# The third lane of the expert loop works its blocks from the last one backwards

## The reference

```python
x = x + L0_xattn(layernorm(x), ctx)      # 16 heads, 722 context rows
x = x + L0_ffn(layernorm(x))             # mixture of experts, below
x = x + L1_xattn(layernorm(x), ctx)
x = x + L1_ffn(layernorm(x))             # ternary weights, 4096 hidden

# L0_ffn: H=1024, E=32 experts, K=4 per token, I=512
logits = x @ gate_w.T + gate_b
topk_logits, topk_idx = top_k(logits, 4)
weight = softmax(topk_logits)
# for each (token, expert) pair:
gate, up = x @ w_gate[e] + b_gate[e], x @ w_up[e] + b_up[e]     # clipped at 7
act  = (up + 1) * gate * sigmoid(1.702 * gate)
y    = sum over the 4 experts of weight * (act @ w_down[e] + b_down[e])
```

## Time and profile before

| | us |
|---|---|
| median of 3 runs | 3518.92 (3517.94 to 3521.68) |
| the profiled execution's own time | 3516.27 |
| its span in the trace | 3514.5 |
| TensorE busy (PE) | 3425.6, 97% |
| VectorE busy (DVE) | 1634.5, 47% |

### The profile page before, as it was taken

How to read it: one execution, slowest core, us unless ns; L and a number is a source line. 1 busy time by engine, 2 the same in 40 slices (tenths; PEclk the granted TensorE clock), 3 DMA queues, 4 the chain that set the end, 5 groups by cost and what they waited for, 6 DMA issues and landing times.

```text
span 3514.5 us, 43051 instructions
## 1 busy us (share of the span) xinstructions
PE 3425.6 (97%) x16460; PEld 1797.4 (51%) x16461; DVE 1634.5 (47%) x1978; ACT 863.7 (25%) x1256; POOL 744.6 (21%) x709
## 2 busy tenths in 40 slices
PE   7999999999999789999999989999999999999999
PEld 4565565566456333333333346556565565554554
DVE  8764474565466431111111146446255365661651
ACT  2330131032023211111111125335154252220110
POOL 4200400400320012212222210000000002780860
PEclk9999999999999989999999999999999999999999
DMA  7631231132123196898888975436355251430420
GB/s 224 225 100 53 63 87 47 68 101 64 49 69 123 77 369 211 303 381 313 285 293 315 368 238 168 134 132 183 100 161 155 85 160 56 149 137 2 160 90 38
DMA packets 93173, 556.64 MB, mean 158 GB/s; under 512 B 11304, under 2 KB 11440, under 8 KB 74992
## 3 DMA queue, kind: packets, MB, share of 16 engines
q1 hardware_dynamic: 58432, 445.28, 35.5%
q0 software_dynamic: 31392, 93.76, 10.3%
q10 hardware_dynamic: 3216, 15.68, 1.5%
HBM read 517.62 MB, written 40.71 MB: 159 GB/s over the span
## 4 chain that ended last, share of the span: by engine, by line
PE 86%; DMA 4%; DVE 3%; ACT 1%; issue 1%; SPq 0%; POOL 0%; DVEq 0%; POOLq 0%; ACTq 0%
PE PS L967 15%; PE PS L1950 11%; PE PS L2284 10%; PE PS L1114 9%; PE PS L924 8%; PE PS L1974 6%; PE PS L2310 5%; PE PS L953 4%; DMA W<-in_W 4%; PE PS L819 4%; PE PS L836 3%; PE PS L903 2%; PE PS L1050 2%; PE PS L851 2%; PE PS L977 1%; PE PS L1942 1%
## 5 line engine op out<-in xcount | busy, mean ns | idle before, releaser
L967 PE MATMUL PS<-Sb,kvN 121*128 121x400 f32 (+1 forms) x1536 | 536.7, 499 | 0.0
L1950 PE MATMUL PS<-W,hT 128*64 128x512 f32 x2208 | 503.5, 598 | 12.1 <-DMA W<-in_W 9.2
L967 PEld LDWEIGHTS PS<-Sb,kvN 121*128 121x128 f32 (+1 forms) x1536 | 286.7, 190 | 205.9 <-issue 2.4
L2284 PE MATMUL PS<-xh,wq 128*128 128x400 f16 x2048 | 347.1, 332 | 1.8 <-DVE xh L1342 1.8
L2059 DVE TENSOR_TENSOR gu<-PS,bias 128x512 f32<-128x512 f32 x69 | 47.7, 692 | 629.6 <-PE PS L1950 602.3
L924 PE MATMUL PS<-kvT,wkr 128*128 128x363 f32 x1024 | 340.4, 475 | 0.0
L1114 PE MATMUL PS<-wb,ctxl 128*128 128x512 f32 x768 | 331.0, 592 | 0.0
L2240 POOL TENSOR_SCALAR gtq<-stg,thr 128x1024 f16<-128x1024 f32 x96 | 287.4, 3011 | 170.4 <-DMA stg<-in_F 142.8
L1518 POOL TENSOR_TENSOR qrope<-qrope,rt 128x400 f32<-128x400 f32 x156 | 157.6, 1034 | 719.2 <-DVE rt L1380 712.8
L1950 PEld LDWEIGHTS PS<-W,hT 128*64 128x64 f32 x2208 | 154.8, 137 | 299.8 <-issue 296.1
L2284 PEld LDWEIGHTS PS<-xh,wq 128*128 128x128 f16 x2048 | 200.2, 98 | 148.0 <-DVE xh L1342 2.3
(11 more groups left out here) (290 smaller groups left out, 3777.4 us busy)
## 6 DMA issues: line engine op xcount, KB each, us to landing
W<-in_W SPq DMA_DIRECT2D x98, 2048.0 KB, 12.5
stg<-in_F SPq DMA_DIRECT2D x32, 1536.0 KB, 6.4
kvT<-kvT_d SPq DMA_DIRECT2D x64, 726.0 KB, 4.3
kvN<-kvN_d SPq DMA_DIRECT2D x64, 726.0 KB
absin<-in_F POOLq DMA_DIRECT2D x48, 512.0 KB, 4.0
hn<-in_F POOLq DMA_DIRECT2D x48, 512.0 KB, 4.8
wb<-in_WB SPq DMA_DIRECT2D x8, 2560.0 KB, 9.2
wc_h<-in_WC SPq DMA_DIRECT2D x32, 576.0 KB, 4.7
```

Of the source, the lines that this page charges most:

```text
L967: mm = nc.tensor.matmul(PS[:, value_bank(b) + dc, 0:GW], kvN[b % 2][0:k, lc, dc * P:(dc + 1) * P], Sb[b % 2][0:k, lc, :], start=lc == 0, s ...
L1950: mm = nc.tensor.matmul(PS[g * BS:(g + 1) * BS, 2 + u % 2, :], hT2[k][:, c, half * BS:(half + 1) * BS], W2[:, q, o:o + N1], start=c == 0, ...
L2284: mm = nc.tensor.matmul(PS[:, 4 * q + 2 * w + half, 0:HALF], wq[q][:, w, c, :], xh[part][:, c, half * HALF:(half + 1) * HALF], start=c == ...
```

## The change

Lanes 0 and 1 keep their blocks. Lane 2 works block 67 - 1 - r in round r: it begins with the last block, and so always with expert 31, and goes down to block 44. Because that expert is known in advance, its gate tile is issued before the routing is known, as soon as `hnm` is stored and transposed, in one piece; SP then waits for `first_e` for lane 1 alone. The 31 loads in the loop stay 31, with a load's first step now being, in lane 2, that of the expert's last block. The expert that straddles the lanes 1 and 2 is loaded in both (`cut`, `cut_e`, `cut_t`, in the place of the last expert's entry). On these inputs the steps at which the 31 loads are first needed are:

```diff
-FIRST_INC = (2 * DN_INC, GU_INC, GU_INC + 16)
+FIRST_INC = (2 * DN_INC, GU_INC, GU_INC)
...
+    back = np.arange(P) % NQ_W == NQ_W - 1
+    c[:, C_BACK] = back
+    c[:, C_BACK + 1] = np.where(back, 0, np.arange(P) % NQ_W)
+    c[:, C_BACK + 2] = np.where(back, -1 - np.arange(P) // NQ_W, np.arange(P) // NQ_W)
...
-            link(dve, ts(bcol[:, :], sq, rounds[:, :], sr, ALU.mult, ALU.add))
+            n_blocks = tend[:, E - 1:E]
+            is_back, sq_f, sr_f = (cst[:, C_BACK + i:C_BACK + i + 1] for i in range(3))
+            link(dve, ts(bcol[:, :], sq_f, rounds[:, :], sr_f, ALU.mult, ALU.add))
+            ts(c_back[:, :], n_blocks, float(NQ_W), -2.0, ALU.mult, ALU.add)
+            ts(c_start[:, :], n_blocks, float(NQ_W), 2.0, ALU.mult, ALU.add)
+            link(dve, stt(bcol[:, :], is_back, n_blocks, bcol[:, :], ALU.mult, ALU.add))
+            stt(c_back[:, :], rounds[:, :], float(NQ_W), c_back[:, :], ALU.mult, ALU.add)
...
-            link(dve, stt(queue, bst[:, :], rounds2[:, :], mine[:, :], ALU.is_ge, ALU.add))
-            link(dve, ts(start[:, :], queue, wrap[:, :], None, ALU.mult))
-            link(dve, stt(start[:, :], bst[:, :], float(NQ_W), start[:, :], ALU.mult, ALU.add))
+            link(dve, stt(cut[:, :], bst[:, :], rounds2[:, :], cut[:, :], ALU.is_lt, ALU.mult))
...
+            link(dve, ts(tail_at[:, :], tail_at[:, :], -float(NQ_W), c_start[:, :], ALU.mult, ALU.add))
+            link(dve, tt(tail_at[:, :], tail_at[:, :], start[:, :], ALU.subtract))
+            link(dve, stt(tail_at[:, :], bst[:, :], rounds2[:, :], tail_at[:, :], ALU.is_ge, ALU.mult))
+            link(dve, tt(start[:, :], start[:, :], tail_at[:, :], ALU.add))
...
+            sp.wait_ge(sem("moe_st"), 16 * MT)
+            sp.wait_ge(sem("ln_tp"), ln_count("moe", "tp", MT))
+            load_gate_up(E - 1, 2)
+            load_bias(E - 1, 2)
             sp.wait_ge(sem("m_first"), 1)
-            sp.wait_ge(sem("moe_st"), 16 * MT)
-            firsts = [0]
-            for q in range(1, NQ_W):
-                e = sp.value_load(first_e[0:1, q:q + 1], min_val=0, max_val=E - 1)
-                if q == 1:
-                    load_gate_up(e, q)
-                else:
-                    sp.dma_start(W2[:, q, 0:W2_A], A["W2"][e, :, 0:W2_A]).then_inc(sem(FIRST_G[q]), 16)
-                    sp.wait_ge(sem("m_hs0"), 16)
-                    sp.dma_start(W2[:, q, W2_A:W2_D], A["W2"][e, :, W2_A:W2_D]).then_inc(sem(FIRST_G[q]), 16)
-                load_bias(e, q)
-                firsts.append(e)
+            second = sp.value_load(first_e[0:1, 1:2], min_val=0, max_val=E - 1)
+            load_gate_up(second, 1)
+            load_bias(second, 1)
+            firsts = (0, second, E - 1)
```

More of the change, by code:

```diff
@@ L104 @@
 C_SPARE = C_HD + 1
-C_FOLD = C_SPARE + 1
+C_BACK = C_SPARE + 1
+C_FOLD = C_BACK + 3
 C_N = C_FOLD + TW[-1]
@@ L312, in build @@
         nt = p0.put("nt", [P, E])
-        tend = p0.put("tend", [P, E])
+        tend = p3.put("tend", [P, E])
         bst = p3.put("bst", [P, E])
@@ L333, in build @@
         cols = p3.put("cols", [P, 5])
+        cut = p3.put("cut", [P, E])
+        tail_at = p3.put("tail_at", [P, E])
+        cut_t = p3.put("cut_t", [P, E])
+        cut_e = p3.put("cut_e", [P, E])
+        c_start = p3.put("c_start", [P, 1])
+        cut_1 = p3.put("cut_1", [P, 3])
         slot = p0.put("slot", [P, TOPK, MT])
@@ L337, in build @@
         que_f = p0.put("que_f", [P, TOPK * MT])
+        back_f = p0.put("back_f", [P, TOPK * MT])
+        c_back = p0.put("c_back", [P, 1])
         row_f = p0.put("row_f", [P, TOPK * MT])
@@ L1608, in route_vector @@
             link(dve, vt.tensor_reduce(rounds[:, :], rcmp[:, :], AX, ALU.add))
-            sq, sr = cst[:, C_SQ:C_SQ + 1], cst[:, C_SR:C_SR + 1]
+            sq = cst[:, C_SQ:C_SQ + 1]
             ts(rounds2[:, :], rounds[:, :], 2.0, None, ALU.mult)
             ts(wrap[:, :], rounds[:, :], -float(NQ_W), 1.0, ALU.mult, ALU.add)
-            link(dve, ts(bcol[:, :], sq, rounds[:, :], sr, ALU.mult, ALU.add))
+            n_blocks = tend[:, E - 1:E]
[5 more added lines that the diff above has]
+            stt(c_back[:, :], rounds[:, :], float(NQ_W), c_back[:, :], ALU.mult, ALU.add)
             link(dve, ts(ended[:, :], tend[:, :], bcol[:, :], None, ALU.is_le))
@@ L1634, in route_vector @@
             link(dve, vt.tensor_copy(blk_f[:, :], srow_i[:, :]))
-            ts(que_f[:, :], blk_f[:, :], rounds[:, :], None, ALU.is_ge)
+            ts(back_f[:, :], blk_f[:, :], -2.0 * NQ_W, c_back[:, :], ALU.mult, ALU.add)
+            ts(que_f[:, :], blk_f[:, :], rounds[:, :], wrap[:, :], ALU.is_ge, ALU.mult)
             link(dve, stt(row_f[:, :], blk_f[:, :], -float(BS), sl, ALU.mult, ALU.add))
-            link(dve, stt(que_f[:, :], blk_f[:, :], rounds2[:, :], que_f[:, :], ALU.is_ge, ALU.add))
-            link(dve, ts(que_f[:, :], que_f[:, :], wrap[:, :], None, ALU.mult))
+            link(dve, stt(back_f[:, :], blk_f[:, :], rounds2[:, :], back_f[:, :], ALU.is_ge, ALU.mult))
+            link(dve, tt(que_f[:, :], que_f[:, :], back_f[:, :], ALU.add))
             link(dve, stt(blk_f[:, :], blk_f[:, :], float(NQ_W), que_f[:, :], ALU.mult, ALU.add))
@@ L1679, in route_vector @@
             vt.tensor_copy(vals[:, 0, :], cst[:, C_EIX:C_EIX + E])
+            vt.tensor_copy(tail_at[:, :], tend[:, :])
+            ts(cut[:, :], tend[:, :], rounds2[:, :], None, ALU.is_gt)
             link(dve, ts(mine[:, :], bst[:, :], rounds[:, :], None, ALU.is_ge))
-            link(dve, stt(queue, bst[:, :], rounds2[:, :], mine[:, :], ALU.is_ge, ALU.add))
-            link(dve, ts(start[:, :], queue, wrap[:, :], None, ALU.mult))
-            link(dve, stt(start[:, :], bst[:, :], float(NQ_W), start[:, :], ALU.mult, ALU.add))
+            link(dve, stt(cut[:, :], bst[:, :], rounds2[:, :], cut[:, :], ALU.is_lt, ALU.mult))
+            link(dve, vt.memset(cut[:, E - 1:E], 0.0))
+            stt(queue, bst[:, :], rounds2[:, :], mine[:, :], ALU.is_ge, ALU.add)
+            stt(cut_t[:, :], tend[:, :], n_blocks, cut[:, :], ALU.subtract, ALU.mult)
+            stt(cut_e[:, :], cst[:, C_EIX:C_EIX + E], -float(E - 1), cut[:, :], ALU.add, ALU.mult)
+            link(dve, ts(start[:, :], mine[:, :], wrap[:, :], None, ALU.mult))
+            vt.tensor_reduce(cut_1[:, 0:1], cut[:, :], AX, ALU.add)
+            vt.tensor_reduce(cut_1[:, 1:2], cut_t[:, :], AX, ALU.add)
+            link(dve, vt.tensor_reduce(cut_1[:, 2:3], cut_e[:, :], AX, ALU.add))
+            stt(start[:, :], bst[:, :], float(NQ_W), start[:, :], ALU.mult, ALU.add)
+            tt(tail_at[:, E - 1:E], tail_at[:, E - 1:E], cut_1[:, 1:2], ALU.add)
+            tt(vals[:, 0, E - 1:E], vals[:, 0, E - 1:E], cut_1[:, 2:3], ALU.add)
+            link(dve, tt(cut_1[:, 0:1], cut_1[:, 0:1], is_back, ALU.mult))
+            link(dve, ts(tail_at[:, :], tail_at[:, :], -float(NQ_W), c_start[:, :], ALU.mult, ALU.add))
+            link(dve, tt(tail_at[:, :], tail_at[:, :], start[:, :], ALU.subtract))
+            link(dve, stt(tail_at[:, :], bst[:, :], rounds2[:, :], tail_at[:, :], ALU.is_ge, ALU.mult))
+            link(dve, tt(start[:, :], start[:, :], tail_at[:, :], ALU.add))
             ts(vals[:, 2, :], start[:, :], -float(NQ_W - 1), 1.0, ALU.add, ALU.max)
@@ L1687, in route_vector @@
                          start[:, :].unsqueeze(1).to_broadcast([P, E, E]), ALU.is_gt))
-            ts(mine[:, :], queue, sq, None, ALU.is_equal)
+            link(dve, ts(mine[:, :], queue, sq, None, ALU.is_equal))
+            stt(mine[:, E - 1:E], cut_1[:, 0:1], 0.0, mine[:, E - 1:E], ALU.is_equal, ALU.mult)
             link(dve, vt.tensor_reduce(ordn[:, :], later[:, :, :], AX, ALU.add))
@@ L1692, in route_vector @@
             link(dve, ts(ordn[:, :], ordn[:, :], sq, None, ALU.subtract))
+            ts(cut[:, :], cut[:, :], is_back, ordn[:, E - 1:E], ALU.mult, ALU.mult)
             link(dve, tt(mine[:, :], mine[:, :], ordn[:, :], ALU.mult))
+            link(dve, tt(mine[:, :], mine[:, :], cut[:, :], ALU.add))
             link(dve, stt(mine[:, :], mine[:, :], sq, here[:, :], ALU.add, ALU.mult))
```

## The result

The changed kernel takes 3544.56 us (median of 4 runs, 3540.07 to 3547.11) against 3518.45 us before on the same chip: a ratio of 1.0073, 95% interval [1.0061, 1.0085]. The forecast was 3544. The profiled execution took 3540.07 us, the fastest of the four, so the two traces differ by 23.8 us, a little less than the medians (26.1).

The account below looks back on a forecast made before the run. TensorE, 86% of the last chain, bounds the kernel; only its weight waits can move. Loop -1.0 + 1.5 + 10.05 + 13.1 = +23.65, start +1.3: +25.0 us on 3516.27, 3541.2, or 3544 on the median's scale; range 3531 to 3556.

Parts of the forecast that it names:

- account of runs: Expert loop: in close loads each takes 18.4 us against 11.25 us a step; TensorE waits for the difference, +23.65 us in all.
- Steps 51 and 64 to 67: Ends of two late runs of loads: +10.05 us of waits over 50 and 51, +13.1 us over 63, 64 and 67.
- step 29: End of the five loads at steps 24 to 29: 6.0 us of waits, the same as before, difference 0.
- W: TensorE's wait in k loads, steps a to b: 0.5 + 18.4 (k-1) + 19.0 - [11.25 (b-a+3) - 3.65] us.
- A term that was missing: Steps 36 and 37: no wait was forecast; loads at 36, 37, 38 become 36, 37, and 0.98 us goes.
- early tile: Lane 2's gate tile at the loop's start: TensorE never waited for it, so issuing it early is worth nothing by itself.
- VectorE's tables: Before step 1: added table instructions 3.5 us and routing about 0.5 us delay `gw`; +1.3 us comes through, bounds 0 to 3.
- The gather: First gather of tokens, behind TensorE's 7.13 us idle: landing earlier helps step 0 only if `gate_places` comes earlier; nothing counted.
- The rival of slow restarts: After the waits at 51, 64 and 67, TensorE restarts at a low clock, three times 1.75 us: +5, 3549; chance 0.13.
- The rival of a low load price: Queue gives every load in 15.9 us, so runs of loads wait little: -0.3 us, 3518.6, not slower; chance 0.05.
- The rival of short intervals: Two new runs, 48 to 51 and 61 to 67, at 17.0 us a load: +14.5 us, 3533; chance 0.12.
- The rule: HBM to SBUF transfers bound at about 358 GB/s: 19.6 us a load, about 3553; the prediction kept 18.4 us.

Follow-up runs that it names:

- renumbered orders: Kernel before, code untouched, lane 2's experts renumbered in the host's weight layout: 3519.23 us (26, 27, 29, 30, 28, 31) and 3555.07 us (30, 26, 29, 31, 28, 27).
- light loads: Loop loads bring only half of each half gate tile, so the layer isn't computed: 3508.27 us on the changed kernel, 3507.5 us on the kernel before.
- early tile alone: Kernel before, forward order, with only lane 2's first gate tile (expert 25) issued early as in the change: 3517.59 us, ratio 1.0003.
- tables alone: Kernel before plus 25 idle VectorE instructions in the places of those the change adds: 3520.01 us, ratio 1.0007.
- spread order: Kernel before, code untouched, lane 2's experts renumbered 26, 27, 29, 30, 28, 31: 3519.23 us; with the gather issued before the scatter, 3511.62 us.

## Why the prediction was right

**The account of runs** was right in mechanism and, on the whole, in size: excess of 32.7 us in the loop against a forecast of 32.85 in all. The agreement of these two totals flatters it: as a difference to the kernel before it forecast +23.65 and got +20.7, since by the same count that loop has 12.0 us, and not 9.2. The renumbered orders, the light loads and the early tile alone each confirm one part of it: the same code with another order moves the time by 37 us, and with half the gate bytes the two orders take the same time.

**Sizes that were off.** Steps 51 and 64 to 67 were 2.4 and 2.0 us cheaper, step 29 gave 4.3 for 6.0. Put into W, the measured terms give each of them: 0.3 us and not 0.5 from the half product to the issue; 53.2 for the three intervals before step 51, 90.4 for the five before step 67 (I had 92), 72.6 for the four before step 29 (73.6); and 18.1, 18.1 and 17.8 us from the last issue to the second half, where I had 19.0. That makes 7.7, 11.1 and 4.3 us. Before step 51 it is the second interval that is short (16.0 us); I had seen that for three loads and not carried it to four. Before step 67 none is (17.8, 17.8, 18.5, 18.1, 18.2). The run of five loads also varies between executions: in four traces with the old order it costs 4.8 to 7.1 us, in three with the reversed lane 3.7 to 5.7.

**A term that was missing**, 5.7 us at step 36: the prediction read SP's queue only. GpSimd's scatters and gathers share the full engines, and in the stretch of steps 24 to 37, nine loads in 14 steps, they fell behind. The trace before had the sign of it: its scatters between 1501.94 and 1579.96 follow each other in 12.1 to 13.8 us, more than a step, and only the dense stretch ended before a gather was late. The missing term and the loads priced too high cancelled, 5.7 against 6.1 us; that the median came within 1 us of the forecast is in part this luck.

**The start.** The early tile was worth nothing, as said. I had VectorE's tables as what is late next, +1.3 us. Net of the 2.75 us from before the routing, step 1 starts 0.95 us later. That can't be told from no effect: from the instruction ahead of the routing to step 1 it is 65.7 us after, and 64.6 to 65.9 us in the six traces (before and five runs) with the code of before in this part. The rows after:

```profile
1245.34 1.97 PE L1977 MATMUL PS<-cst,hs 128*128 128x128 f32 x8 [6.12 <-DMA hs<-h_d,idxc]
1247.23 5.79 PE L1985 MATMUL PS<-W,hT 128*64 128x512 f32 x16
...
1255.14 3.65 PE L1985 MATMUL PS<-W,hT 128*64 128x512 f32 x16
1258.72 0.68 PE L2025 MATMUL PS<-gw,dup 128*128 128x84 f32 x4
1259.33 1.03 PE L2032 MATMUL PS<-cst,cols 128*1 128x128 f32 x8
1263.24 3.65 PE L1985 MATMUL PS<-W,hT 128*64 128x512 f32 x16 [2.88 <-issue]
```

The gather did land 1.0 us earlier for TensorE's idle (6.12 against 7.13), the price that I had left at nothing. `gate_places` at 1258.72 follows the second half with no idle: step 0's slow first half, 5.79 us, took the time. But `gw` was done only at 1258.51, so the tables would have held it nearly as long. From their first instruction to `gw` they take 9.7 us (from 1248.80), 3.0 more than before (1245.45 to 1252.19), and the routing ahead of them 0.6 more, where I had 3.5 and 0.5; in the run with the tables alone TensorE waited for them. Step 1's first half then ran in 3.65 us and not in 5.35, 1.7 us given back. Neither is the change's: in the spread order, with the code of before, the two took 5.77 and 3.65 us.

**The rival of slow restarts** fell in its size of 5 us, but not wholly. The first halves at 1845.64 and 2001.30 do take 5.26 and 5.93 us after 4.99 and 5.73 us of idle, with a granted clock of 0.69 and 0.61, and the second halves behind them have 1.9 and 2.3 us of excess. At step 51 the second half tile was the later one, as argued: it landed at 1851.70, and TensorE went on at 1851.84. At step 64 it wasn't. The tile landed at 2006.42 (17.2 us after its issue at 1989.23), while TensorE came to it at 2007.96 with no idle. At full speed it would have come at 2005.64 and gone on when the tile was there, so about 1.4 us of step 64 are the slow restart (an estimate from these times), which I had at nothing; 0.7 us at step 37 is another one. The rival of a low load price fell too: no interval in the changed kernel is under 15.9 us, and the first of each run is 17.8. The rival of short intervals, 17.0 us in the new runs, is nearer, but they average 17.7 and 18.1.

**The rule** of the Trainium skill ("DMA: Bandwidth & Descriptors", "Where 436 GB/s comes from") that such transfers are bound at about 358 GB/s does not hold here, on one core: 383 and 401 GB/s in the saturated windows after. The ceiling of 435 wasn't reached in them.

**What stays open**: why the stage before the routing varies by up to 3.9 us; whether the table instructions cost 0 or 2 us, which is under what these runs tell apart; and how much of the late gather is the place behind the scatter and how much the scatters' delay.

## What to carry to other kernels

Where weights are loaded while they are used, the average (31 loads of 18.4 us in 69 steps of 11.25) says little: list the steps at which loads are first needed, take each run of close ones, and compare its loads' time with its steps' time. Here lanes that reached their short pieces together cost more than the early load could save, and the order of the list was worth more than the code around it. And look at each queue that shares the full engines: what stands behind a slow, serial transfer in program order is late with it.

## What the runs showed of the hardware

- With the 16 DMA engines full of weight loads, a scatter with addition of 256 KB was issued 12.6 to 14.3 us after the one it waited for (nine in a row from 1517.94 in the spread order). A gather of 512 KB landed 8.4 to 16.7 us after its issue in such stretches of the spread order and of the changed kernel; the two that stopped TensorE took 16.7 and 15.6 (the second from 1656.18). At the start of the loop, with a DMA share of 0.52, it took 4.2 us (1241.10 to 1245.34 in the changed kernel).
- A share of 1.00 is not one rate: 435 GB/s with weight loads alone, 382 to 401 with scatters and gathers among them.
- After 5 to 6 us without work TensorE's next 16 matmuls took 5.3 to 5.9 us in place of 3.6, at a granted clock of 0.69 and 0.61. This cost nothing at step 51, where a transfer was the later one, and about 1.4 us at step 64. A shorter idle time can do it too: 2.05 us at step 7 of the spread order brought 5.35 us, while 2.34 us at step 29 of the changed kernel brought 3.65.
